# Four chained layers on one core: causal zeros two heads at a time, half of the maxima sent ahead in two chunks, and new engine orders

## What is computed

```python
    att = jnp.einsum('bhtd,bhsd->bhts', q, k) * scale          # A0: 16 heads of 8
    att = jnp.where(causal[None, None], att, jnp.finfo(att.dtype).min)
    att = jax.nn.softmax(att, axis=-1)
    y = jnp.einsum('bhts,bhsd->bhtd', att, v)
...
    h = jax.nn.silu(_tlin(x, w1_w, w1_s)) * _tlin(x, w2_w, w2_s)   # F0
    h = jax.nn.gelu(_tlin(h, h1_w, h1_s), approximate=False)
    h = jax.nn.gelu(_tlin(h, h2_w, h2_s), approximate=False)
    return _tlin(h, w3_w, w3_s)
...
    energy = jnp.einsum('bqhe,bkhe->bqhk', q, k)                # A1
    attn = jax.nn.softmax(energy, axis=-1) / sqrt(E)
    out = jnp.einsum('bihv,bvhd->bihd', attn, v)
...
    x = _layernorm(x + _L0_attn_ref(...)); x = _layernorm(x + _L0_ffn_ref(...))
    x = _layernorm(x + _L1_attn_ref(...)); x = _layernorm(x + _L1_ffn_ref(...))
```

## Time and profile before

| | us |
|---|---|
| median of 3 runs | 967.79 |
| lowest and highest | 964.33, 969.79 |
| the profiled execution | 969.01 |
| its span, first to last instruction | 966.9 |
| PE busy in the span | 899.3 |
| DVE, ACT, POOL busy | 672.6, 489.5, 163.1 |
| mean granted TensorE clock | 0.972 of full |

### The profile page before, as it was taken

The page is one execution under the profiler, slowest core; times in us unless marked ns, Lnnn a source line. Parts: engine busy times, 40 slices in busy tenths (PEclk is TensorE's granted clock), DMA queues, the critical chain, the costliest instruction groups (busy, mean ns, idle before and its releaser), DMA issues. The chain is left out here.

```text
span 966.9 us, 19090 instructions
## 1 busy us (share of the span) xinstructions
PE 899.3 (93%) x7072; PEld 692.5 (72%) x7072; DVE 672.6 (70%) x2371; ACT 489.5 (51%) x951; POOL 163.1 (17%) x261
## 2 busy tenths in 40 slices
PE   4687999999999999999999999999999999999995
PEld 3454787876677876678777876788767887778654
DVE  5656648749897489872898579945898659446732
ACT  0043554386555564546647365535555575462461
POOL 1022112002310041101420023101320123011001
PEclk9998999999999998999999999999999999999897
DMA  9403032302231034201232024120432022010200
GB/s 308 116 29 110 19 93 67 107 22 62 85 99 53 12 84 127 74 19 40 65 112 67 19 73 116 42 72 19 121 94 58 2 67 67 1 56 24 78 7 12
DMA packets 48899, 65.16 MB, mean 67 GB/s; under 512 B 5608, under 2 KB 42728, under 8 KB 44232
## 3 DMA queue, kind: packets, MB, share of 16 engines
q1 hardware_dynamic: 46744, 58.61, 21.2%
q10 hardware_dynamic: 2064, 5.34, 1.5%
HBM read 48.46 MB, written 14.68 MB: 65 GB/s over the span
## 5 line engine op out<-in xcount | busy, mean ns | idle before, releaser
L516 ACT ACTIVATE prob<-ps_s 128x384 f32<-128x384 f32 (+1 forms) x512 | 249.8, 549 | 114.3 <-PE ps_s L828 89.8
L637 DVE TENSOR_REDUCE top<-ps_s 128x2 f32<-128x512 f32 (+1 forms) x280 | 181.7, 684 | 71.2 <-PE ps_s L805 56.7
L828 PE MATMUL ps_s<-qrow,krow 75*128 75x256 bf16 (+1 forms) x1024 | 161.9, 269 | 7.8 <-DMA qrow<-tsplit 5.0
L628 DVE CUSTOM_DVE_ANT_0 ps_s<-ps_s,above 128x128 f32<-128x128 f32 x448 | 146.0, 388 | 26.6 <-PE ps_s L805 18.3
L805 PE MATMUL ps_s<-krow,qrow 72*128 72x256 bf16 x768 | 148.9, 286 | 8.4 <-DVE top L628 3.9
L846 PE MATMUL ps_g<-prob,v 128*32 128x256 f32 (+1 forms) x2048 | 126.3, 373 | 3.0 <-POOL prob L470 1.7
L828 PEld LDWEIGHTS ps_s<-qrow,krow 75*128 75x128 bf16 x1024 | 90.1, 101 | 48.1 <-ACT prob L516 18.0
L915 PE MATMUL ps_g<-glu,wh 128*128 128x256 f32 x512 | 118.7, 386 | 0.0
L915 PE MATMUL ps_g<-hid,wh 128*128 128x256 f32 x512 | 116.4, 381 | 0.0
L463 POOL TENSOR_TENSOR ln_rstd<-ln_var,minus_half 128x2 f32<-128x2 f32 x64 | 45.3, 712 | 416.8 <-DVE ln_var L686 416.1
L915 PEld LDWEIGHTS ps_g<-glu,wh 128*128 128x128 f32 x512 | 96.5, 193 | 13.3 <-issue 0.4
(11 more groups left out here) (94 smaller groups left out, 1193.8 us busy)
## 6 DMA issues: line engine op xcount, KB each, us to landing
qrow<-scratch SPq DMA_DIRECT2D x30, 576.0 KB
krow<-scratch SPq DMA_DIRECT2D x90, 192.0 KB
scratch<-split SPq DMA_DIRECT2D x96, 128.0 KB, 1.9
xt<-in_xt SPq DMA_DIRECT2D x16, 128.0 KB, 2.4
x<-in_x SPq DMA_DIRECT2D x16, 128.0 KB, 2.3
wh<-in_wh ACTq DMA_DIRECT2D x1, 2048.0 KB, 13.6
out<-xout SPq DMA_DIRECT2D x16, 128.0 KB, 2.1
qrow<-tsplit SPq DMA_DIRECT2D x96, 8.0 KB, 1.8
```

Source lines behind the costliest of these rows:

```text
L516: nc.scalar.activation(prob[s][:, j % 2, g, 0:wide], ps_s2[:, (GROUP * j + g) % PSUM2, 0:wide], ACT.Exp, scale=1.0 / float(np.sqrt(np.floa ...
L628: done = nc.vector.tensor_tensor_reduce(out=bank[:, g * wide:(g + 1) * wide], in0=bank[:, g * wide:(g + 1) * wide], in1=above[:, 2 * P - w ...
L637: nc.vector.tensor_reduce(out=dst, in_=src, axis=AX, op=ALU.max, negate=True).then_inc(maxed[s], 1)
L828: done = nc.tensor.matmul(bank[:, kb * SEQ:(kb + 1) * SEQ - q0], krow[s][n % DEEP[s]][0:ROWSM, h, kb * P:(kb + 1) * P], qrow[s][n % DEEP[s ...
```

## The change

Three things change. Lines in this section are those of the changed kernel where order prints them.

First, `causal` of A0 works on two heads instead of four: there are two such steps for each group, the first after two exponentials, the second after four. `values` still waits for both.

Second, the halved chunks get a step `early`: when the maxima of the first eight heads are there, PE transposes them by themselves, VectorE splits them (on partitions 32 to 39) and SP sends three rows for eight heads. `maxima` of these chunks then sends the other eight heads. pass2 waits for the early rows at its first head, and for the late ones at its ninth.

Third, the five order strings are new throughout, with new letters for the same steps.

```diff
 HALVED = {A0: 0, A1: CHUNKS - 1}
+HALF = HEADS // 2
+CAUSAL = 2
 SEQUENCE = {
     "dve": (
-        "abuaccccccccccccdccccccccccccdbagikqgbccaccccccccqccidckccccqccccccqcbdasgviwckxccscqccvyyqyyyyyyybgyyay"
+        "abvcacccccccdcccceccccccccccccebahjlrbhccaccccccccrccjelcccccccrcccrccbeathwjxylccctcwrcczzrzzzzzzzbzzha"
...
-            "causal": [(j,) for j in range(GROUPS)],
+            "causal": [(j, g) for j in range(GROUPS) for g in range(1, GROUP, 2)],
...
+        top_early = {A0: top[A1], A1: top[A0]}
+        tsplit = {s: sb(f"tsplit{s}", [32 + HALF, PARTS, SEQ], BF16) for s in (A0, A1)}
+        trest = {s: sb(f"trest{s}", [32 + HALF, SEQ]) for s in (A0, A1)}
...
             def maxima(s, n, g):
                 sp.wait_ge(tparts[s], 4 * n + 4)
+                there = slice(HALF, HEADS) if n == HALVED[s] else slice(0, HEADS)
                 for i in range(PARTS):
-                    sp.dma_start(qrow[s][n % DEEP[s]][ROWS + i:ROWS + i + 1, :, :], tsplit[s][:, i, :]).then_inc(trows[s], DMA)
+                    sp.dma_start(qrow[s][n % DEEP[s]][ROWS + i:ROWS + i + 1, there, :],
+                                 tsplit[s][0:HALF if n == HALVED[s] else HEADS, i, :]).then_inc(trows[s], DMA)
+
+            def early(s, n, g):
+                sp.wait_ge(early_parts[s], 4)
+                for i in range(PARTS):
+                    sp.dma_start(qrow[s][n % DEEP[s]][ROWS + i:ROWS + i + 1, 0:HALF, :],
+                                 tsplit[s][32:32 + HALF, i, :]).then_inc(early_rows[s], DMA)
...
-            def mask(s, n, j):
+            def mask(s, n, j, g):
 
-                pool.wait_ge(exped[A0], S2 * n + GROUP * (j + 1))
+                pool.wait_ge(exped[A0], S2 * n + GROUP * j + g + 1)
...
-                diag = prob[A0][:, j % 2].rearrange("p h (k q) -> p h k q", k=2)[:, :, :, 0:P]
+                diag = prob[A0][:, j % 2, g - 1:g + 1].rearrange("p h (k q) -> p h k q", k=2)[:, :, :, 0:P]
                 nc.gpsimd.affine_select(out=diag, in_=diag, compare_op=ALU.is_ge, fill=0.0, base=0,
-                                        pattern=[[0, GROUP], [0, QB], [1, P]],
+                                        pattern=[[0, 2], [0, QB], [1, P]],
...
+            def early(s, n, g):
+                src, t, r = ps_g[32:32 + HALF, g, 0:SEQ], tsplit[s][32:32 + HALF], trest[s][32:32 + HALF, :]
+                dve.wait_ge(early_full[s], 1)
+                nc.vector.tensor_copy(t[:, 0, :], src).then_inc(early_parts[s], 1)
+                dve.wait_ge(early_parts[s], 1)
+                nc.vector.tensor_tensor(r, src, t[:, 0, :], ALU.subtract).then_inc(early_parts[s], 1)
+                dve.wait_ge(early_parts[s], 2)
+                nc.vector.tensor_copy(t[:, 1, :], r).then_inc(early_parts[s], 1)
+                dve.wait_ge(early_parts[s], 3)
+                nc.vector.tensor_tensor(t[:, 2, :], r, t[:, 1, :], ALU.subtract).then_inc(early_parts[s], 1)
...
+            def early(s, n, g):
+                pe.wait_ge(maxed[s], S1[s] * n + S1[s] // 2)
+                last.wait(pe, g)
+                for qb in range(QB):
+                    done = nc.tensor.transpose(ps_g[:, g, qb * P:(qb + 1) * P], top_early[s][:, qb, :], ident[:])
+                done.then_inc(early_full[s], 1)
+                last.used(g, early_parts[s], 2)
+
             def pass2(s, n, j, g):
-                if j == 0 and g == 0:
+                if j == 0 and g == 0 and n == HALVED[s]:
+                    pe.wait_ge(early_rows[s], PARTS * DMA)
+                if j == (HALVES if n == HALVED[s] else 0) and g == 0:
                     pe.wait_ge(trows[s], PARTS * DMA * n + PARTS * DMA)
...
             def values(s, n, j, g):
                 if s == A0:
-                    pe.wait_ge(causal, GROUPS * n + j + 1)
+                    pe.wait_ge(causal, CAUSAL * (GROUPS * n + j + 1))
```

125 lines of the change are left out of this document (66 added, 59 removed).

## The result

The changed kernel takes **955.32 us** in the median of 4 runs (954.10 to 958.25), against 968.79 us of the kernel before on the same chip. The ratio is 0.9872 with a 95% interval of 0.983 to 0.9914. The forecast was 966; the measured time lies 0.3 us inside the low end of its range of 955 to 974, and the gain, 13.5 us, is eight times the 1.7 us of the sum. It has the size of the rival that the orders win more than the new steps, for which 960 or 954 us were worked out.

The account below looks back on a forecast made before the run. PE, busy 899.3 of 966.9 us, was taken as the bound, leaving its idle time and low clock to win. The terms 1.3 - 1.07 - 1.0 - 0.9 = -1.7 us took the median 967.79 to 966 us, range 955 to 974.

Parts of the forecast that it names:

- the orders win more than the new steps: Rival: fewer middle waits and no low-clock episode at 380 us give 954 us, half of that 960; chance 0.33.
- its own signs of being wrong: Middle's PE busy time or waits differing by over 5 us, low-clock episodes coming or going, or first pass2 at 50.
- Head, up to the first pass2: Program start: VectorE's later split of chunk 1 delays its fetch, first pass2 at 47.9 instead of 46.61, 1.3 us lost.
- With the same 3.3 us the fetch begins at 37.5: Head: chunk 1's last piece issued by about 34.2, fetch after the earlier 3.3 us delay, 3.1 us later than before.
- parking lands faster: Head: lower bound of the loss before the first pass2, 0.7 us instead of 1.3.
- From chunk 1's maxima on: Head, to chunk 0's turn: 0.66 us lost, 0.94 (cast) and 0.79 (wait) gained, together 1.07 us gained.
- The halved zeroing: GpSimd's causal zeroing: 639 ns instead of 1101; 0.5 us of PE's waits and 0.5 of VectorE's holds, 1.0 us gained.
- the expected loss is near half: Middle: zeroings holding up VectorE cost PE about 1.0 us in two waits; half of that, 0.5 us, goes.
- The collisions stay: Rival: zeroings hold VectorE as long in sum and meet the cast again, 967.4 us; within the forecast's chance of 0.5.
- more lockouts by more instructions: Shared VectorE and GpSimd ports: 64 more zeroings and 64 more additions are more chances of lockout; by it alone 967.4 us.
- Tail: Near the end: early rows let pass2 run ahead of the merge, 1.3 us of waits go, transposes cost 0.44, 0.9 gained.
- The rest of the orders: All five engine strings, mainly the middle: no reason for a sign, 0, between 5 us lost and 8 gained.

Follow-up runs that it names:

- e6: The changed kernel once more, with only one empty line ahead of it: 952.90 us, 0.9847 of the kernel before.
- e11: The kernel before once more, unchanged: 968.35 us, ratio 1.000.
- e12: The changed kernel without GpSimd's 128 causal zeroings, the tiny additions releasing PE instead (computation incomplete): 949.14 us, 0.9829 of the kernel before.
- e1: The changed kernel with whole zeroing (four heads at a time) again, new orders and early step kept: 960.97 us, 0.9912 of the kernel before.
- e9: The changed kernel's new orders with neither halved zeroing nor early step: 967.23 us, 1.0007 of the kernel before.
- e10: The kernel before, old orders and whole zeroing, with the early step alone added: 965.16 us, 0.9964 of the kernel before.
- e2: The changed kernel without the early step, new orders and halved zeroing kept: 966.75 us, 0.9969 of the kernel before.
- e7: The changed kernel with the early step only in chunk 0 of the first attention, not in chunk 15 of the second: 961.72 us, 0.9903 of the kernel before.

## Why the prediction was right and wrong

**The time was in the range, but the sum behind it was not, and that is luck:** 0.3 us less and it had been outside, as the 952.90 us of `e6` are. By two of its own signs of being wrong the prediction failed: the middle's PE busy time differs by 10.5 us, over the 5 named, and the low-clock episode at 380 us went. By its steps:

*Head, up to the first pass2: +1.3 forecast, -0.4 measured (46.25 instead of 46.61).* The split began at 31.84, forecast 31.87. The failed step is "With the same 3.3 us the fetch begins at 37.5": SP issued the last piece at 34.09 and the fetch began 1.5 us later, at 35.55. What was carried over from before was the time of three pieces issued together, not of one; that this made the difference is argued and not tested. The bound that was named, parking lands faster, reached only to +0.7, so it was too narrow as well. The -0.4 itself says little: in `e11`, the kernel before again, the first pass2 came at 47.66.

*Between the two, nothing forecast, -1.4 measured.* Chunk 1's maxima were turned at 59.98 instead of 61.70, 1.7 us earlier, of which the first pass2 brought 0.4. The new orders did the rest; the sum had no term for it.

*From chunk 1's maxima on: -1.07 forecast, -1.35 measured* (the head's -3.07 less the 1.72 up to there). From the transposes to the next pass2 it is 5.25 us against 6.33, the cast takes 0.28 us, and the wait of 0.79 for the turn is gone. The three parts of this term were not measured apart, so that its sum was right says only that.

*The halved zeroing: -1.0 forecast.* A zeroing takes 637 ns (639 forecast), and PE's waits for it fell from 1.7 to 0.5 us. That is the part that was seen. The failed step is that "the expected loss is near half", with two waits as its measure: the whole is 10 to 13 us of VectorE's time, not some 2, and halving took a fifth of it with the old orders and next to nothing with the new ones, as the rival *The collisions stay* had it. In four pairs of kernels the halving was nevertheless worth 0.33 to 0.65%, about 4 us. The Trainium skill, "SBUF — State Buffer", section "SBUF: two separate sides", has GpSimd and those VectorE instructions that need the shared ports exclude each other for whole instructions; `e12` agrees in the direction that matters here, 10 us of VectorE's time come back when GpSimd's zeroings go. Its argument against the change, more lockouts by more instructions, was borne out in number: 31 lengthened instructions instead of 17. Of the 4 us the profiles show 1.0 us in PE's waits for zeroing (1.5 us in `e1` and `e9`, 0.5 in the changed kernel) and 0.3 to 0.8 us of its own time in the middle (768.4 to 768.1 with the new orders, 770.6 to 769.8 with the old); where the rest lies stays open.

*Tail: -0.9 forecast, -0.9 measured (63.6 against 64.5).* Both waits are gone. But the mechanism was only half told: in the old orders the early step near the end is worth nothing (`e10`: 65.0), and in the new ones it saves some 8 to 10 us (71.4 to 72.7 in `e2`, `e7` and `e9`, 60.4 to 64.0 with it) that they would otherwise lose. I had read in the order that seven heads of pass2 moved ahead of the merge, and asked what the early rows win there, not what that order would cost without them.

*The rest of the orders: 0 forecast.* This is the step that missed the result. The middle became 10.4 us shorter in the two profiles: 2.1 us of PE's own time, which all profiles show, and 8.5 us of half clock, of which on average 4.9 go with the orders and the rest was luck of this pair. The waits, in which I had looked for the orders' gain ("a third of the middle's waits"), grew by 1.2 us on average. The strings do not read alike, as the prediction had it: 29 instead of 20 neighbouring pairs of `values` were there to be counted. The `values` matmuls hold 1.3 us of the 2.1; what makes the rest of PE's own time shorter was not taken apart. Nor were ScalarE's 12 fewer table loads (busy 489.5 us before, 471.8 after), for which the prediction counted nothing. The rival had the right size, and one of its two parts: the episode at 380 us went (8.5 us of half clock in this pair), a third of the waits did not.

**Put together** from averages of the profiles in the table: head -5.2 us (early -3.0, orders -2.2), middle -5.8 by the orders, end -0.4 by orders and early step together (62.3 on average in five profiles, against 62.7 in the three of the old orders without it). That is 11.4, and the halving adds what of its 4 us does not lie in these already. The two comparisons gave 12.4 and 14.8 us by their ratios. The range held the time because its lower end was taken from the rival, not from the bounds of the sum.

## What to carry to other kernels

When a new order comes with a new step, cost the new order without the step too: a step that looks small can be what lets the order stand. On an engine that is 97% busy look for the order's gain in the engine's own time, in which kinds of matmul follow each other, and in its clock, not only in its waits; and take several profiles, since the clock's part comes and goes. When an engine that is idle 80% of the time lengthens the instructions of another, what it costs is read from the other's busy time with and without it, not from the few waits that name it.
